# A graph layer on one core: h[dst] picked out of the node pass on TensorE, scatters that add, all 16 rows of a chunk normalised on ScalarE

## What is computed

```python
h = jnp.maximum(_layernorm(x, axis=-1), 0.0)
concat = jnp.concatenate([h[src], h[dst], edge_attr], axis=-1)      # 96 + 96 + 64
gated = jax.nn.sigmoid(concat @ W_e + b_e) * jax.nn.softplus(concat @ W_n + b_n)
h_new = jax.ops.segment_sum(gated, dst, num_segments=n)
edge_count = jnp.clip(segment_sum(ones, dst), 1.0, None)[:, None]
out = x + (h + h_new / edge_count)
```

## Time and profile before

| | us |
|---|---|
| median of 3 runs | 865.22 |
| lowest, highest | 864.51, 868.50 |
| the profiled execution, its own time | 866.81 |
| span of the profiled execution | 865.0 |

### The profile page before, as it was taken

The page is one execution under the profiler, slowest core; times in us unless marked ns, Lnnn a source line. Parts: engine busy times, 40 slices in busy tenths (PEclk is TensorE's granted clock), DMA queues, the critical chain, the costliest instruction groups (busy, mean ns, idle before and its releaser), DMA issues.

```text
span 865.0 us, 10598 instructions
## 1 busy us (share of the span) xinstructions
PE 569.3 (66%) x2360; PEld 447.4 (52%) x2360; DVE 560.8 (65%) x2397; ACT 583.2 (67%) x1475; POOL 668.3 (77%) x598
## 2 busy tenths in 40 slices
PE   0497775784666466988764665489966664569861
PEld 0376554564554355666553554367655543456650
DVE  5799977567756775677567756775577557754550
ACT  3699988757775777577757775777577756775440
POOL 4787778777777777777777877787778777877774
PEclk9999987768788777555788788755577788775575
DMA  6766655544554455445544554455445543532200
GB/s 215 218 208 192 190 183 147 189 126 125 152 187 125 125 155 184 125 124 149 189 128 123 152 186 127 125 147 189 129 124 147 187 129 125 159 99 80 72 31 23
DMA packets 67032, 125.23 MB, mean 145 GB/s; under 512 B 38167, under 2 KB 39049, under 8 KB 66968
## 3 DMA queue, kind: packets, MB, share of 16 engines
q1 hardware_dynamic: 47390, 96.48, 36.8%
q0 software_dynamic: 18816, 27.77, 10.7%
q10 hardware_dynamic: 762, 0.30, 0.1%
HBM read 77.50 MB, written 48.17 MB: 145 GB/s over the span
## 4 chain that ended last, share of the span: by engine, by line
POOL 74%; issue 20%; DMA 2%; POOLq 1%; DVE 1%; PE 0%; ACTq 0%; SPq 0%
POOL edge_x L324 53%; POOL out L341 22%; DMA out<-node_out 1%; DMA index_rows<-in_src 1%; POOLq L341 1%; DMA edge_x<-in_x,gather_idx 0%; POOLq L339 0%; DVE node_out L637 0%; DVE stats L663 0%; DVE final L575 0%; POOLq L321 0%; DVE softplus L705 0%; PE trans_ps L760 0%; ACTq L245 0%; DVE gather_idx L500 0%
## 5 line engine op out<-in xcount | busy, mean ns | idle before, releaser
L324 POOL DMA_INDIRECT edge_x<-in_x,gather_idx x392 | 469.1, 1197 | 128.2 <-issue 119.2
L398 ACT ACTIVATE node_out<-node_x,shift,rstd 128x96 f32<-128x96 f32 x686 | 279.0, 458 | 1.7 <-DVE shift L615 1.7
L793 PE MATMUL trans_ps<-ident,concat 128*128 128x128 f32 x392 | 92.7, 414 | 259.6 <-ACT concat L433 259.6
L341 POOL DMA_INDIRECT out<-final,scatter_idx x196 | 197.9, 1010 | 59.7 <-issue 58.5
L663 DVE BATCH_NORM_STATS2 stats<-edge_x 128x6 f32<-128x96 f32 x392 | 67.4, 245 | 258.6 <-DMA edge_x<-in_x,gather_idx 258.6
L809 PE MATMUL z_ps<-weights,concat_t 128*128 128x192 f32 x784 | 220.8, 414 | 0.0
L793 PEld LDWEIGHTS trans_ps<-ident,concat 128*128 128x128 f32 x392 | 73.9, 216 | 276.1 <-ACT concat L433 257.0
L809 PEld LDWEIGHTS z_ps<-weights,concat_t 128*128 128x128 f32 x784 | 151.1, 227 | 56.0 <-issue 56.0
L405 ACT ACTIVATE log_var<-var 128x24 f32<-128x24 f32 x51 | 11.4, 223 | 239.0 <-DVE var L685 239.0
L433 ACT ACTIVATE concat<-edge_x,shift,rstd 128x96 f32<-128x96 f32 x392 | 145.7, 456 | 2.7 <-DVE shift L615 0.7
L557 DVE BATCH_NORM_STATS2 stats<-node_x 128x6 f32<-128x96 f32 x784 | 142.6, 242 | 0.0
(11 more groups left out here) (68 smaller groups left out, 373.4 us busy)
## 6 DMA issues: line engine op xcount, KB each, us to landing
node_x<-in_x SPq DMA_DIRECT2D x49, 768.0 KB, 5.8
out<-node_out SPq DMA_DIRECT2D x49, 768.0 KB, 7.5
dst_across<-in_dst SPq DMA_DIRECT2D x48, 256.0 KB, 7.1
edge_x<-in_x,gather_idx POOLq DMA_INDIRECT x392
concat<-in_edge_attr SPq DMA_DIRECT2D x48, 128.0 KB, 6.3
out<-final,scatter_idx POOLq DMA_INDIRECT x196, 2.2
dst_across<-in_dst SPq DMA_DIRECT2D x1, 212.0 KB, 3.6
index_rows<-in_dst SPq DMA_DIRECT2D x2, 64.0 KB
```

Of the source, the lines that this page charges most:

```text
L324: nc.gpsimd.indirect_dma_start(out=edge_x[u][:, t, side, :], out_offset=None, in_=x, in_offset=bass.IndirectOffsetOnAxis(ap=gather_idx[:, ...
L341: nc.gpsimd.indirect_dma_start(out=out, in_=final[j % FINALS][:, t, :], in_offset=None, out_offset=bass.IndirectOffsetOnAxis(ap=scatter_id ...
L398: last = nc.scalar.activation(node_out[u][:, r, :], node_x[u][:, r, :], ACT.Relu, bias=shift[us][:, c:c + 1], scale=rstd[us][:, c:c + 1])
L793: last = nc.tensor.transpose(trans_ps[h][:, t, b, :], concat[uk][:, 2 * h + t, b * P:(b + 1) * P], ident[:, :])
```

## The change

The gather of x[dst] goes. A node chunk is laid out with node r x 128 + p in row r of partition p, so a block of 128 consecutive nodes is one row r of `node_out`. Since dst is sorted, the edges whose targets lie in a block are consecutive, at most WINDOW = 64 of them. After ScalarE has normalised a chunk, TensorE multiplies each of its 16 blocks (96 x 128, stationary) with a 0/1 matrix of 128 x 64 (`onehot`: is the low part of dst equal to the partition's number), and h[dst] of 64 edges comes out transposed, in `pick_ps`. ScalarE copies 336 columns of it (half a chunk) to their place in `dst_t`. Where a window begins is data: a table, made in the prologue from one more gather and nine comparisons, is read into registers of TensorE (16 entries per chunk), ScalarE (2) and SyncE (2).

With it come:

- z has three products per tile: `src_t` with w_src (the bias is a row of ones in it), `dst_t` with w_dst, `attr_t` with w_attr. Only x[src] and the attributes are transposed: 4 and 2 products instead of 8.
- x[dst] + h[dst] is no longer added by VectorE: the scatter adds (`compute_op=ALU.add`) to what the node pass has stored, so `base` and its addition go, and `final` is one product of 384 columns.
- All 16 rows of a chunk are normalised on ScalarE (the relu moves there too); `node_out + node_x` becomes a plain sum, and it waits for `pick_done`, since the picks read `node_out` first.
- SyncE loads `low_across` (2 x 400 columns, spread over 128 partitions) for `onehot`, one chunk per step.
- The second comparison covers only the last 32 edges of the previous tile (`same_prev`, 32 x 4 x 32).
- The pieces of a chunk's load and store are rows of 384 bytes. LEAD is 3 instead of 2, scatters follow after LAG = 5 steps instead of 7, FINALS is 4 instead of 6.

```diff
+            def picks(d, h, at):
+                wait(pe, pick_out, 2 * d + h)
+                for b in range(BLOCKS):
+                    a = at[h * BLOCKS + b]
+                    last = nc.tensor.matmul(pick_ps[0:D, bass.ds(a, WINDOW)], node_out[d % NS][:, h * BLOCKS + b, :],
+                                            onehot[d % 2][:, h, bass.ds(a, WINDOW)], start=True, stop=True)
+                last.then_inc(pick_done, 1)
...
+            def pick_columns(d, h, at):
+                wait(act, pick_done, 2 * d + h + 1)
+                nc.scalar.activation(dst_t[0:D, bass.ds(at, REACH)], pick_ps[0:D, 0:REACH], ACT.Copy).then_inc(pick_out, 1)
...
+            def one_hot(n):
+                wait(dve, low_loaded, 32 * (n + 1))
+                wait(dve, pick_done, 2 * (n - 1))
+                nc.vector.tensor_scalar(onehot[n % 2][:, :, :], low_across[:, :, :], lane[:, 0:1], None,
+                                        ALU.is_equal).then_inc(onehot_done, 1)
...
+                if runs_step(d):
+                    wait(dve, node_norm_done, d + 1)
+                    wait(dve, pick_done, 2 * d + 2)
+                    nc.vector.tensor_tensor(node_out[d % NS][:, :, :], node_out[d % NS][:, :, :], node_x[d % NS][:, :, :],
+                                            ALU.add).then_inc(node_sum_done, 1)
...
+            def load_low(n):
+                first, second = (first_at(sp, first_row[0:1, 2 * n + h:2 * n + h + 1]) for h in range(2))
+                wait(sp, onehot_done, n)
+                for h, at in ((0, first), (1, second)):
+                    sp.dma_start(low_across[:, h, :],
+                                 low_flat[bass.ds(at, SPAN)].partition_broadcast(P)).then_inc(low_loaded, 16)
...
                     for t in range(TB):
                         nc.gpsimd.indirect_dma_start(
                             out=out, in_=final[j % FINALS][:, t, :], in_offset=None,
                             out_offset=bass.IndirectOffsetOnAxis(ap=scatter_idx[:, j * TB + t:j * TB + t + 1], axis=0),
-                            bounds_check=NODES - 1, oob_is_err=False).then_inc(scattered[j % FINALS], 16)
+                            bounds_check=NODES - 1, oob_is_err=False, compute_op=ALU.add).then_inc(scattered[j % FINALS], 16)
```

More of the change, by code:

```diff
@@ L29, with build @@
 SLACK = AHEAD * CHUNK - (TB - 1) * (CHUNK // TB)
-assert STEPS * TB == TILES and STEPS * CHUNK >= NODES > (STEPS - 1) * CHUNK
-def build(nc, x, src, dst, edge_attr, w_e, b_e, w_n, b_n, out, count_table):
+HALVES = 2 * STEPS
+BLOCKS = R // 2
+WINDOW = 64
+REACH = 336
+SPAN = REACH + WINDOW
+LOOK = 4 * P
+assert STEPS * TB == TILES and STEPS * CHUNK >= NODES > (STEPS - 1) * CHUNK and LOOK - P > REACH
+def build(nc, x, src, dst, edge_attr, w_e, b_e, w_n, b_n, out, count_table, dst_pad, low_pad):
     ctx = ExitStack()
@@ L81, in build @@
+        attr = [sb(f"attr{u}", [P, TB, DE]) for u in range(NS)]
+        src_h = [sb(f"src_h{v}", [P, TB, D]) for v in range(2)]
+        dst_across = [sb(f"dst_across{v}", [P, TB, P], I32) for v in range(2)]
+        low_across = sb("low_across", [P, 2, SPAN])
+        onehot = [sb(f"onehot{v}", [P, 2, SPAN]) for v in range(2)]
         final = [sb(f"final{u}", [P, TB, D]) for u in range(FINALS)]
-        real, ahead = (final[u][:, :, :].rearrange("p t d -> p (t d)")[:, 0:2 * P].rearrange("p (b e) -> p b e", b=2)
-                       for u in range(FINALS - 2, FINALS))
@@ L96, in build @@
         correction = sb("correction", [P, ROWS])
[L97 to L103, removed]
+        src_t = sb("src_t", [P, TB, P])
+        attr_t = sb("attr_t", [P, 2, P])
+        log1p = [sb(f"log1p{v}", [P, TB, 2 * D]) for v in range(2)]
@@ L311, in _, with step @@
                                     pattern=[[-1, P]], channel_multiplier=1).then_inc(const_done, 1)
-            nc.gpsimd.affine_select(out=later[:, :], in_=ones[:, :], compare_op=ALU.is_gt, fill=0.0, base=0,
-                                    pattern=[[-1, P]], channel_multiplier=1).then_inc(const_done, 1)
-            def step(i, o, u):
+            def step(i):
                 if runs_step(i):
                     if i == 0:
-                        pool.wait_ge(gather_idx_done, 2)
-                    wait(pool, base_done, i - NS + 1)
+                        pool.wait_ge(src_idx_done, 1)
+                    wait(pool, edge_norm_done, i - NS + 1)
@@ L598, in newton @@
+            def newton(k, chunk):
+                u = k % NS
                 wait(dve, rough_done, k + 1 + LEAD)
@@ L633, in step @@
+                if now:
+                    last = node_stats(c, 3, R)
+                if runs_step(n):
+                    one_hot(n)
                 if runs_step(d):
                     wait(dve, node_norm_done, d + 1)
[L636 to L638 removed]
@@ L664, in step @@
+                    for r in range(TB):
+                        last = nc.vector.bn_stats(stats[:, r, :], edge_x[i % NS][:, r, :])
                 if runs_rows(i):
@@ L785, in step @@
+                if runs_step(d):
+                    if d == 0:
+                        pe.wait_ge(place_loaded, 32)
+                        pe.wait_ge(ones_done, 2)
+                    pe.load(place_regs, place_row[0:1, d * R:(d + 1) * R])
+                    at = [pe.snap(r, min_val=0, max_val=REACH) for r in place_regs]
+                    wait(pe, node_norm_done, d + 1)
+                    wait(pe, onehot_done, d + 1)
+                    picks(d, 0, at)
                 if runs_step(k):
@@ L798, in step @@
+                    last.then_inc(attr_trans_done, 1)
+                if runs_step(d):
+                    picks(d, 1, at)
                 if runs_step(m) and not ends(i, 1):
@@ L812, in step, with later_sums @@
                     sums(i - 2)
-            steps(step, 2)
+            for i in range(-LEAD, STEPS + 2):
+                step(i)
             pe.wait_ge(flag_done, 1)
             bad = pe.value_load(flag[0:1, 0:1], min_val=0, max_val=1)
-            def tile_sums(t, n):
+            def later_sums(n):
                 pe.wait_ge(r_diag_done, n + 1)
```

786 lines of the change are left out of this document (486 added, 300 removed).

## The result

The changed kernel takes **950.07 us** (median of 4 runs, 949.51 to 951.62) against 865.8 (median of 4, 864.51 to 868.5): ratio 1.0972, 95% interval [1.0941, 1.1002]. It is slower by a tenth, where 746 us was forecast with a range of 660 to 905. The profiled run took 950.48 us with a span of 948.7, at a mean granted clock of 0.792 of full speed.

The account below looks back on a forecast made before the run. GpSimd, the busiest engine, was to give way to TensorE as the bound at 14.0 us a step; 102 us of fill and tail plus 46 such steps gave 746 us, range 660 to 905.

Parts of the forecast that it names:

- the closing of the loop in the paragraph on DMA: SyncE's queue: comparison, VectorE sum, issues, table entries, low_across transfer, next comparison; 11.4 to 12.6 us, under TensorE's bound.
- TensorE's 14.0: TensorE's work per step, 14.0 us (ends 11.3 and 17.4), taken as the new bound; picks at 0.32 us each.
- the sum's own form: Whole kernel: span is 102 + 46 x P, with P the steady step in us; 746 us at P = 14.0.
- the two issues after the sum at 0.8 us: SyncE: two issues following VectorE's sum in the loop through low_across, 0.8 us together.
- my 0.023: DMA engines: 0.023 us per small packet, so a chunk's load and store cost 5.9 us after, 7.0 before.
- the 1.3 us of the sum: DMA: transfer time for the two low_across loads in SyncE's loop, 1.3 us beside 5.9 for the chunk.
- The rule of the Trainium skill: DMA: transfers below 512 bytes miss line rate and are read, modified and written; doubled store packets would give 8.8 us.
- rival (a): TensorE not the bound, picks near 0.15 us; GpSimd, ScalarE, SyncE's loop take over: P = 12.3, 668 us; chance 0.24.
- Rival (b): TensorE stays at 1.2 GHz: step about 21 us, 1068 us, slower than before; chance 0.15.
- Rival (c): SyncE's queue bounds: dearer stores, full register reads, interleaved gathers; P = 15.5 to 16, 815 to 838 us; chance 0.18.
- The 0.16 for slower: Whole kernel: chance 0.16 of a slower result, beside 0.82 for faster by over 0.5% and 0.02 within 0.5%.
- The fill: Start of the kernel, ahead of the 46 full steps: first gathers, comparisons, low_across and picks, about 50 us.

Follow-up runs that it names:

- the 766.85 us version: Changed kernel with the dst_across load and the low_across loads both moved ahead of SyncE's wait for the chunk's sum: 766.85 us, 0.7926 of before on that chip.

## Why the prediction was wrong

**The step that failed** is the closing of the loop in the paragraph on DMA. I followed SyncE's queue as far as `low_across`, found 11.4 to 12.6 us and set it under TensorE's 14.0. Two lines further in the same step of the same queue stands the load of `dst_across`. The prediction says nothing of it. It is issued after everything that waits for VectorE's sum, and VectorE's next step begins with it. With it the loop is 5.9 + 6.1 + 6.1 = 18.2 us, and 102 + 46 x 18.2 = 939, by the sum's own form, against a span of 948.7. The run with this load at the head (799.25) shows the step.

**Why it had cost nothing before.** In the kernel before the load also stands last, and it took 7.0 us to land, more than after. But it had four buffers (NS), and step i loaded it for the edges of step i - 3. The changed kernel has two buffers and loads for i - 7. The traces show what that does: before, the first issue is at 10.3 us and the first comparison at 57.4, the last ones at 789.8 and 839.7, so about 50 us of lead; after, they are at 95.5 and 101.8, and at 912.9 and 924.3. By these leads the loop needs both, the last place and the lost lead. Giving back the lead without changing the order was not tried.

**Terms inside the loop.** SyncE's part was undersized: the two issues after the sum at 0.8 us measured 0.4 + 1.6, the issues of `low_across` at 0.7 measured 2.3 to 2.6, the table entries at 0 to 1.2 took 1.1 to 1.8 (493.30 to 494.43, and 511.46 to 513.21). Moving the load alone therefore left a step of 15.05 us and not 12. I had multiplied packets by a duration and asked whether the DMA engines have the time. They do: 1560 packets of the changed kernel passed in the 2 us from 512 to 514, 2 x 16 / 1560 = 0.0205 us each, and my 0.023 was good. Stores cost hardly more than loads: 752 packets passed from 497 to 498 us, after the load's 5.2 us to landing were over. What I didn't ask is who stands behind the burst. The reader finds it in the table by stretch: DMA share 0.80 to 1.25 from 495 to 503 us, while VectorE is idle, and 0.24 and 0.08 in two stretches in which it works throughout. Nor did the two loads of `low_across` pass in the 1.3 us of the sum: their 1.6 KB pieces fill the stretch from 499 to 501 and part of the next. The rule of the Trainium skill that I weighed there (DMA: Bandwidth & Descriptors, Specifications) isn't seen in these packets of 384 bytes, at 0.0205 us each.

**The adding scatter.** I took 1.01 us and kept 2.0 as the other end. It measures 1.58 in the changed kernel, and 1.84 with the loop out, where it most likely decides: the 766.85 us version has 4 x (1.84 + 0.30) + 4 x (1.04 + 0.30) = 13.9 us of GpSimd in a step, beside a mean step of 14.0 (chunk loads from 102.89 to 635.14, 38 steps). The forecast's value of 14.0 for TensorE is near to it only by coincidence.

**TensorE.** Picks 0.17 to 0.19 us at full clock (8 in 1.3 to 1.5), not 0.32; a tile of z 0.98 (513.21 to 514.19), not 1.36: each of its three products follows the one before at 0.33. So 16 x 0.18 + 3.92 + 1.86 + 0.7 + 0.9 = 10.3 us: rival (a) had TensorE right. Rival (b) didn't come: the clock is 0.792 on the whole, 0.50 at the head of each step and 1.00 later in it, and TensorE holds 3% of the chain, so here this costs little.

**Rival (c)** named the right queue with the wrong transfer and gave at most 852. Its upper end of P = 16 lay just under the 16.6 at which the sum crosses the time of before, so one more DMA in the loop was enough to change the sign. The 0.16 for slower was too little for a queue that I hadn't followed to its end.

**The fill** and the tail were 102 us in the sum. With the mean step of 18.34 the sum gives 102 + 46 x 18.34 = 946, 3 us under the span of 948.7: together they were right, and whether each was is not shown.

## What to carry to other kernels

When a change adds DMAs behind a wait on one queue, follow that queue to the end of the step, and for each issue ask how early its reader needs it; an issue that stands last and is needed first in the very next step closes a loop over the whole step. When buffers are cut, ask the same of every load that lived on them. In these traces a short transfer issued behind a burst landed only when what its queue had been given before it was through. Where the DMA engines alternate between full and idle and an engine's idle time ends at a DMA, move the issue before touching anything else: here that one move was worth 151 us, and the two 183.

## What the runs showed of the hardware

- The issue of a DMA on SyncE is not a constant: the store of 2048 pieces took 1.58 us behind the load of 2048 pieces, 0.43 with 128 pieces each, and 4.34 with `low_across` just ahead; the load of `dst_across` took 0.43 or 3.06 by what stood before it.
- Packets of 384 bytes pass at 0.0205 us each on each of 16 engines, reads and writes mixed, at 297 GB/s (512 to 514 us of the changed kernel). The pieces of 1.6 KB that spread `low_across` over the partitions pass at 122 GB/s (499 to 501 us).
- An adding scatter of 128 rows of 384 bytes costs GpSimd 1.58 to 1.84 us to issue in the mean, where the plain one costs 1.00 to 1.09; the software queue has 34576 packets with it and 12624 without.
- Reading a table entry into a register takes SyncE 0.27 us and 0.15 for the address behind it; some of these reads took 1.1 to 1.4 in the run in which large pieces are the only edit.
- The granted clock did not simply follow TensorE's share of busy time: 0.839 at 75% in the 766.85 us version, 0.771 at 71% with a third of the z products out, 0.817 at 67% with three scatters as well, 0.884 at 78% with three scatters alone. What sets it is not shown.
- Kernels with plain scatters, that of before among them, showed waits of ScalarE and VectorE on TensorE that no recorded product accounts for (234.7 us in one run; single ones up to 26 us in the kernel before) on the chips of the experiments, while the trace of before on the chip of the result has none. With adding scatters they were 68.5 us or less. What makes them stays open.
